# Own order for the opening of a paged-attention, FFN and adapter kernel, with plain fp32 products for tile 0, page numbers first and bulk loads held back

## The reference

```python
# paged attention, 32 query heads on 8 key heads, D = 128, cache of 512 keys + 128 new ones per batch
q, k, v = x @ Wq.T, x @ Wk.T, x @ Wv.T
q, k = rope(rmsnorm(q, q_norm_w), pos), rope(rmsnorm(k, k_norm_w), pos)     # pos = cache_seqlens + 0..127
kc = k_cache[block_table]; vc = v_cache[block_table]                        # 16 pages of 32 keys
scores = where(valid, q @ concat(kc, k).T / sqrt(D), -1e30)
c = softmax(scores) @ concat(vc, v) @ Wo.T
# FFN that zeroes the 688 of 1376 smallest magnitudes per row
s = silu(c @ w_gate.T); s[lower half by |s|] = 0
x = x + (s * (c @ w_up.T)) @ w_down.T
# adapter by batch, then an int4 layer
x = x + (x @ weight[adapter_ids].T) @ unpack_int4(W).T + b
```

## Time and profile before

| | us |
|---|---|
| three runs | 1374.59, 1374.22, 1374.66 |
| median | 1374.59 |
| span of the profiled execution | 1372.6 |
| PE busy | 1356.7 (99%) |
| DVE busy | 1204.1 (88%) |
| ACT busy | 871.6 (64%) |
| POOL busy | 785.0 (57%) |
| granted PE clock | full in all 40 slices |

### The profile page before, as it was taken

How to read it: one execution, slowest core, us unless ns; L and a number is a source line. 1 busy time by engine, 2 the same in 40 slices (tenths; PEclk the granted TensorE clock), 3 DMA queues, 4 the chain that set the end, 5 groups by cost and what they waited for, 6 DMA issues and landing times.

```text
span 1372.6 us, 23448 instructions
## 1 busy us (share of the span) xinstructions
PE 1356.7 (99%) x8015; PEld 1182.3 (86%) x8015; DVE 1204.1 (88%) x2624; ACT 871.6 (64%) x2224; POOL 785.0 (57%) x813
## 2 busy tenths in 40 slices
PE   8899999999999999999999999999999999999998
PEld 6788888888888888888888888888888888888888
DVE  8999898989898989898989898989899987987783
ACT  7777676767676767676767676767777662222221
POOL 7876766676667666766676667666766510111111
PEclk9999999999999999999999999999999999999999
DMA  6111221111112111211111112112121321111212
GB/s 215 48 53 41 59 55 47 43 59 55 47 43 59 54 47 43 58 55 47 43 59 53 49 42 59 55 47 70 49 72 32 110 96 45 47 47 49 76 40 77
DMA packets 34034, 80.46 MB, mean 59 GB/s; under 512 B 10258, under 2 KB 11538, under 8 KB 32498
## 3 DMA queue, kind: packets, MB, share of 16 engines
q1 hardware_dynamic: 17522, 45.29, 10.5%
q0 software_dynamic: 16384, 33.59, 8.4%
HBM read 76.74 MB, written 2.10 MB: 57 GB/s over the span
## 4 chain that ended last, share of the span: by engine, by line
PE 91%; DVE 5%; ACT 2%; issue 1%; POOL 1%; DMA 0%; DVEq 0%; ACTq 0%
PE proj_ps L111 10%; PE proj_ps L113 10%; PE proj_ps L112 10%; PE turn_ps L770 10%; PE score_ps L113 5%; PE score_ps L112 5%; PE score_ps L111 5%; PE value_ps L111 5%; PE value_ps L112 5%; PE value_ps L113 5%; PE gu_ps L111 3%; PE gu_ps L113 3%; PE gu_ps L112 3%; PE out_ps L1035 2%; PE turn_ps L732 2%; PE turn_ps L739 2%
## 5 line engine op out<-in xcount | busy, mean ns | idle before, releaser
L1286 ACT ACTIVATE probs<-probs,shift,rstd 128x640 f32<-128x640 f32 x256 | 234.4, 917 | 123.3 <-DVE shift L1730 122.2
L561 POOL DMA_INDIRECT kg<-kc,idx x256 | 260.1, 1016 | 83.9 <-issue 78.0
L571 POOL DMA_INDIRECT vg<-vc,idx x256 | 260.0, 1016 | 70.7 <-issue 70.7
L1766 DVE TENSOR_TENSOR pt_lo<-turn_ps,pt_hi 128x512 fp32r<-128x512 f32 x320 | 217.4, 685 | 45.2 <-ACT pt_hi L1292 44.8
L1292 ACT ACTIVATE pt_hi<-turn_ps 128x512 fp32r<-128x512 f32 x320 | 187.5, 593 | 90.6 <-PE turn_ps L770 89.3
L1741 DVE CUSTOM_DVE_ANT_0 probs<-score_ps,mask 128x640 f32<-128x640 f32 x256 | 206.8, 822 | 11.9 <-PE score_ps L113 10.1
L579 POOL TENSOR_TENSOR v_lo<-vg,v_hi 128x512 fp32r<-128x512 f32 x64 | 89.1, 1392 | 207.7 <-ACT v_hi L1257 207.7
L770 PE MATMUL turn_ps<-cst,probs 128*128 128x128 f32 x1280 | 191.5, 272 | 0.7 <-DVE qt_lo L1718 0.7
L111 PE MATMUL proj_ps<-w_hi,xt_parts 128*128 128x512 f32 x496 | 188.9, 381 | 0.0
L770 PEld LDWEIGHTS turn_ps<-cst,probs 128*128 128x128 f32 x1280 | 157.2, 141 | 26.9 <-DVE probs L1759 1.0
L113 PE MATMUL proj_ps<-w_hi,xt_parts 128*128 128x512 f32 x496 | 168.1, 339 | 0.0
(11 more groups left out here) (255 smaller groups left out, 3283.4 us busy)
## 6 DMA issues: line engine op xcount, KB each, us to landing
w_raw<-wqkv SPq DMA_DIRECT2D x28, 384.0 KB, 3.2
wo_raw<-wo SPq DMA_DIRECT2D x32, 256.0 KB, 3.0
wa_sb<-wa SPq DMA_DIRECT2D x7, 1024.0 KB, 4.9
kg<-kc,idx POOLq DMA_INDIRECT x256, 2.6
vg<-vc,idx POOLq DMA_INDIRECT x256
wg_raw<-wg SPq DMA_DIRECT2D x2, 1376.0 KB, 6.1
wu_raw<-wu SPq DMA_DIRECT2D x1, 2752.0 KB, 9.6
wd_raw<-wd SPq DMA_DIRECT2D x1, 2560.0 KB, 12.8
```

What stands on the lines that cost most here:

```text
L561: pool.indirect_dma_start(kg[:, b % 2, c, :], None, kc, bass.IndirectOffsetOnAxis(ap=idx[:, s // B % 2, b * NC + c:b * NC + c + 1], axis=0))\
L571: pool.indirect_dma_start(vg[:, b % 2, c, :], None, vc, bass.IndirectOffsetOnAxis(ap=idx[:, s // B % 2, b * NC + c:b * NC + c + 1], axis=0))\
L1286: act.activation(row, row, ACT.Exp, bias=shift[:, h:h + 1], scale=rstd[:, b % 2, h:h + 1], accum_out=sums[:, h:h + 1])\
L1766: dve.tensor_tensor(pt_lo[:, at, :], turn_ps[1 - j % 2][:, :], pt_hi[:, at, :].bitcast(F32), ALU.subtract).then_inc(p_lo_done[j], 1)
```

## The change

The opening (everything before step 1) gets an order of its own on each engine, and other transfers:

- Tile 0's projections of step 0 are made in plain fp32 from x and w as loaded (`first_q`, `first_kv`), four products each, one per 128 rows as each piece of w lands. w of group 0 is loaded and split in five pieces (`W0_PIECES`). x 0 is split only in step 3, as it is next needed in step 8. Three warm-up products on PE instead of six.
- ACT's queue issues page numbers, the small constants, lengths and the identity; SP begins with x 0.
- SP waits for tile 0's cached keys (`k_in[0]`) before it issues x 2 and 3, x 4 to 7 and the output weights.
- ACT normalises one head of four in step 0 and one in step 1 (`BY_ACT`), and the orders of `steps_ahead` and `first_step` differ on all engines. POOL's tables stand elsewhere.
- The angles are reduced with two terms of 2 pi instead of three, and the lengths are read as integers.

Steps 1 to 63 keep their order, but for x 0's split in step 3.

```diff
-TWO_PI = (6.28125, 0.0019350051879882812, 3.0199157663446503e-07)
+TWO_PI = (6.28125, 0.0019353071795864769)
+W0_PIECES = [(slice(k, k + 1), slice(0, GQ)) for k in range(NK)] + [(slice(0, NK), slice(GQ, GW))]
+BY_ACT = (1, 2)
-FILLED = 6
+FILLED = 3
@@ sync
-                    sp.dma_start(cst[:, :], consts[:, 0:C_KEY]).then_inc(const_in, 16)
-                    sp.dma_start(lens_i[:, :], lens).then_inc(const_in, 16)
-                    sp.dma_start(pages_i[:, :], pages).then_inc(pages_in, 16)
                     sp.dma_start(x_raw[:, 0, :, :], xt_b[:, 0, :, :]).then_inc(x_in[0], 16)
-                    for n, (ks, cols) in enumerate(W_PIECES):
-                        if n == LAST_PIECE:
+                    for n, (ks, cols) in enumerate(W0_PIECES):
+                        if n == len(W0_PIECES) - 1:
...
-                    sp.dma_start(key_no, consts[:, C_KEY:C_ALL]).then_inc(key_in, 16)
-                    sp.dma_start(x_raw[:, 2:B, :, :], xt_b[:, 2:B, :, :]).then_inc(x_in[2], 16)
+                    sp.dma_start(key_no, consts[:, C_KEY:C_ALL]).then_inc(table_in, 16)
+                    sp.wait_ge(k_in[0], NC * 16)
+                    sp.dma_start(x_raw[:, 2:4, :, :], xt_b[:, 2:4, :, :]).then_inc(x_in[2], 16)
+                    sp.dma_start(x_raw[:, 4:B, :, :], xt_b[:, 4:B, :, :]).then_inc(x_in[3], 16)
                     for h in range(REP):
                         sp.dma_start(wo_raw[:, h, :], wo[0, :, h, :]).then_inc(wo_in, 16)
@@ tensor
+                    def first_q():
+
+                        pe.wait_ge(x_in[0], 16)
+                        for k in range(NK):
+                            pe.wait_ge(w0_in[k], 16)
+                            last = pe.matmul(proj_ps[:, :], x_raw[:, 0, k, :], w_raw[:, k, 0:GQ], start=k == 0,
+                                             stop=k == NK - 1)
+                        last.then_inc(q_chunks, Q_CALLS)
...
-                        first_projections()
+                        first_q()
+                        first_kv()
+                        pe.wait_ge(ident_in, 16)
+                        turn_cached_k(0, 0)
+                        project_q(1, 1, 0, (0, 1))
                         project_q(1, 1, 0, (2,))
-                        turn_cached_k(0, 0)
                         project_q(1, 1, 0, (3,))
...
@@ scalar
+                    def normalise(s, b, heads):
+
+                        wait(act, recip_done, s + 1)
+                        for h in heads:
+                            row = probs[:, b % 2, h, :]
+                            act.activation(row, row, ACT.Copy, scale=recips[:, h:h + 1]).then_inc(probs_act_done, 1)
...
+                    act.dma_start(pages_i[:, :], pages).then_inc(pages_in, 16)
+                    act.dma_start(cst[:, C_INV:C_KEY], consts[:, C_INV:C_KEY]).then_inc(const_in, 16)
+                    act.dma_start(lens_i[:, :], lens).then_inc(lens_in, 16)
+                    act.dma_start(ident, consts[:, C_ID:C_ID + P]).then_inc(ident_in, 16)
@@ vector
-                        normalise(0, 0, (1, 2, 3))
-                        maxima(1, 1, (0, 1))
+                        normalise(0, 0, (1,))
+                        normalise(0, 0, (2,))
+                        maxima(1, 1, (0,))
+                        maxima(1, 1, (1,))
                         split_probs(0, 0, 0)
...
                         if s < B - 4:
                             split_x(s + 4)
+                        if s == B - 5:
+                            split_x(0)
```

More of the change, by code:

```diff
@@ L656, in table, with steps_ahead @@
                             ALU.mult).then_inc(pool_tables_done[n], 1)
+                    def steps_ahead():
+                        gather_k(0, 0, 0)
+                        gather_k(1, 1, 0)
+                        norms(0, 0)
+                        gather_v(0, 0)
+                        table(0, 1, 0)
+                        norms(1, 1)
+                        gather_v(1, 1, range(0, NC // 2))
+                        gather_k(2, 2, 0)
+                        split_v(0, 0)
+                        table(0, 1, 1)
+                        table(1, 1, 0)
+                        norms(2, 2)
                     def first_step():
+                        gather_v(1, 1, range(NC // 2, NC))
                         gather_v(2, 2)
@@ L697, in project_q @@
                     def project_q(s, b, g, ks):
-                        if b == 0 and ks[0] in (0, 2):
-                            wait(pe, w_lo_done[ks[0] // 2], g + 1)
+                        if b == 0 and g > 0 and ks[0] in (0, 2):
+                            wait(pe, w_lo_done[ks[0] // 2], g)
+                        if s == 1:
+                            wait(pe, w0_lo_done, ks[-1] + 1)
                         if ks[0] == 0:
@@ L1759, in normalise @@
                             last = dve.tensor_scalar(row, row, recips[:, h:h + 1], None, ALU.mult)
-                        if h == REP - 1:
+                        if h == REP - 1 or s < len(BY_ACT) and h == REP - 1 - BY_ACT[s] + (BY_ACT[s - 1] if s else 0):
                             last.then_inc(probs_done, 1)
                     def split_probs(s, b, j):
-                        wait(dve, p_hi_done[j], s + 1)
+                        wait(dve, p_hi_done, NJ * s + j + 1)
                         at = (b + j) % 2
```

246 lines of the change are left out of this document (120 added, 126 removed).

## The result

| | before | after |
|---|---|---|
| median | 1374.33 (5 runs) | 1378.84 (5 runs: 1374.88 to 1379.75) |
| profiled execution, span | 1374.59, 1372.6 | 1374.88, 1373.1 |
| PE, DVE, ACT, POOL busy | 1356.7, 1204.1, 871.6, 785.0 | 1357.3, 1199.9, 873.4, 782.5 |

The ratio is 1.0026, 95% interval 1.0015 to 1.0037; the median is 4.5 us higher. The change is slower where 3.9 us less was forecast. The first profile caught the shortest of the five executions, so that it says little of the other four. I call them the short and the long course; both are read here.

A forecast was written before the change was run, and what follows sets the result against it. PE's waits, mostly for DVE, before step 1's third value product were taken as the bound. Terms 1.0 - 0.8 + 3.9 - 0.2 = 3.9 us cut span 1372.6 to 1368.7; 2.0 around it gave 1370.7 us, range 1368.0 to 1374.4.

The forecast's parts named there:

- Page numbers first: At the start, page numbers issued earlier: index at 3.4 us instead of 4.06, `rstd` 0.9 us sooner.
- Plain fp32: Tile 0's projections on PE as plain products: worth nothing on the path, with about 1.5 us of cover.
- edits at nothing: Angle reduction, w's five pieces, ACT's DMA issues and identity transfer: all done before 18.8 us, so no cost.
- Held bulk: SP's bulk loads wait for tile 0's keys, which land at about 12.2 us instead of 16.7.
- Rival one: Tile 0's keys don't land sooner despite the hold: 1373.3 us, chance 0.12.
- What the hold makes late: Output weights land at 23.1 us, ACT stands about 1 us at `split_wo`; cost 0, with 1.4 us of cover.
- Rival three: Slower: ACT stands at late output weights; 1375.8 us, or 1378 if PE starves too; chance 0.08.
- DVE, first leg: DVE from 18.8 us to the first `pt_lo`, ending at 36.5 against 36.67: 0.2 us gained.
- DVE, second leg: DVE from the first `pt_lo` to the opening's end: 20.05 us instead of 24.0, ending 4.1 us earlier.
- pair waits: DVE instructions with two SBUF operands stalled by POOL arithmetic: 4.2 us in the opening, to go in the second leg.
- rival two: Stalls of DVE beside POOL's arithmetic come back elsewhere: 1372.8 us, or 1375.9 if all of it hits; chance 0.15.
- the join: Third value product of step 1 on PE, forecast at 59.1 us against 62.98; 0.2 us lost there.

The follow-up runs named there:

- wo_first: The changed kernel with the output weights issued ahead of x 4 to 7 after the hold; 1378.25 us.
- again: The changed kernel run again, nothing edited; 1377.74 us, ratio 1.0023 to the kernel before. Its profile caught a longer execution.
- tables_later: The changed kernel with POOL's tables `qb` and `ka` moved from behind `split_v(0, 0)` to behind `gather_v(2, 2)`; 1374.52 us, ratio 1.0005 to the kernel before.
- tables_late: The changed kernel with tables `qb` and `ka` moved behind `gather_v(1, 1)`, ahead of `norms(2, 2)`; 1528.02 us, ratio 1.0012, on a slow chip (before: 1524.57).
- tables_late2: tables_late once more, on another slow chip; 1487.75 us (kernel before: 1486.35).
- spread_later: tables_later with each of the three tables alone between gathers; 1519.37 us, ratio 0.9973, on a slow chip (kernel before: 1524.16).
- again2: The changed kernel unaltered, run again in the last decision group; 1378.39 us, ratio 1.0027 to the kernel before.
- kb_early: The changed kernel with POOL's table `kb` moved from behind `split_v(1, 1)` to ahead of `gather_k(3, 3, 0)`; 1377.47 us, ratio 1.0020 to the kernel before.
- the fourth group: Runs again2, tables_late3 (tables_late repeated), kb_early and tables_later, on one chip beside the kernel before, which took 1374.26 us.
- before_early2: Second run of the kernel before with tables `qa` and `qb` moved directly behind `split_v(0, 0)`; 1490.22 us, ratio 1.0020, on a slow chip.
- small_on_sp: The changed kernel with page numbers, constants and lengths issued by SP ahead of its bulk instead of by ACT; 1374.48 us.

## Why the prediction was wrong

**What bounds the kernel, and how to count: right.** The rest is fixed from the third value product on; the table above bears it out within 0.4 us either way. PE's busy time is as before within 1 us.

**Page numbers first: wrong.** Index forecast at 3.4, measured 5.12. I took the landing time of a transfer issued ahead of all bulk in the trace of before (2.3 us of waiting) for transfers issued beside it, where the constants took 3.8 us. The same three issued on SP ahead of the bulk give 3.58. `rstd`, and with it `rotate_k(0)`, gained 0.2 instead of 0.9 to 1.0.

**Plain fp32, edits at nothing:** worth 0, as said; the keys' products end at 11.9 (forecast 11), ahead of the cached keys.

**Held bulk: mechanism right, size 1.5 us off.** Keys turned at 13.7, not 12.2. Rival one fell: without the hold the last gather, issued at 10.85, is used at 16.82, and with it 10.79 becomes 13.73.
**What the hold makes late: 1.4 to 2 us off, and harmless.** `wo` split at 25.1 and 24.5 in the two courses, not 23.1. It did not set the end, as said (wo_first), though in the short course DVE stood 0.55 us for tile 2's queries behind it. Rival three, my only way to slower, fell.

**DVE, first leg: this step failed.** I had its first `pt_lo` end at 36.5; it ends at 39.95 and 40.1 in the two courses. In again the 3.6 us are three terms:

- 0.8 from the start, `rotate_k(0)` at 19.64, by the late index.
- 0.7 on the way to the reciprocals, forecast for 31.5 (31.2 by my own terms) and measured at 33.02; DVE waits 0.42 and 0.45 us for scores and ahead of `rot_q` where I had 0.35 in all.
- 2.1 at the bias behind the second maximum of tile 1. It reads two SBUF operands. I priced its wait at 1.1 us, by `v_lo(0)` alone, and it stands 3.18, until POOL is through `v_lo` twice, `qb` and `ka`.

The last one is the step that decides. It is in the sentence "tables `qb` and `ka` run at 36.4 to 38.4, beside maxima and `pt_lo`", which puts them at nothing; but between the maxima stand the biases. So the wait that I saw removed at 40.56 was moved to 36.3, and grew. In the short course DVE comes to the bias later, at 38.05 (it was held 0.55 us for queries and 1.2 us for scores, PE's clock being low from 33.7 to 37.1), stands only 1.31, and ends at the same `ka`. Taking the two tables away behind `v_lo(0)` brings the first leg's pair to 38.37 and gives back 3.9 of 4.1 us (tables_later).

That I counted on the end of the first `v_lo` was not without a row. Before:

```profile
35.66 0.33 DVE L1730 SCALAR_TENSOR_TENSOR shift<-row_max,rstd 128x1 f32<-128x1 f32 x1
```

The bias got through at 35.99, where the first `v_lo(0)` ends, though the second follows at once (35.91). So it did in tables_late, tables_late2, tables_later and spread_later (0.35 to 0.37 us), all with a gather or the norm behind the two `v_lo`. With `qb` and `ka` behind them it waited for `ka`'s end each time (again, again2, wo_first and kb_early: 3.18, 2.67, 3.19 and 2.70 us). Why the same boundary lets it through in one order and not in the other, no run shows.

**DVE, second leg: near in the short course** (20.8 against 20.05, most of it the bias at 56.27, which stands 1.51 beside `v_lo(1)` where 0.7 was allowed), **wrong in the usual one.** The pair waits came back, as rival two said with a chance of 0.15: `v_lo(1)` against the rotation products, 2.7 us over their free length. Its upper price, 1375.9, left out what follows such a wait: PE idles 2.5 us, and the clock falls behind it.

**The sum.** 1.0 - 0.8 + 3.9 - 0.2 became 0.2 - 3.5 + 3.2 and nothing at the join in the short course: the first leg's loss eats the second leg's gain. The long one loses another 3.4 us by the join, of which 2.7 are the rotation products' wait; that the rest goes with PE's idling and its low clock is argued, not shown. What sends an execution into one course or the other stays open.

## What to carry to other kernels

When two engines shut each other out, a moved instruction must be priced against everything that the other engine issues in its new place, small instructions above all. Price the wait up to the end of the whole run of such instructions, not of the first alone: four profiles here waited for it in full, though others got through after the first. Read more than one profile of a kernel whose executions scatter more than those of the kernel before (5 us against 1 in the fourth group): the one profile may be the lucky course. And an earlier engine can be the worse one, since it meets others elsewhere.

## What the runs showed that I had not expected

- DVE's normalisation reads one tensor and a column of factors, and is held by POOL's arithmetic all the same: 4.40 us in before_early2 where one alone takes 0.55. The prediction had only instructions with two SBUF operands. The Trainium skill (SBUF — State Buffer, "SBUF: two separate sides") names DVE instructions in a two-port performance mode beside those with two SBUF inputs; the trace agrees with it as far as the 4.40 us go, though no run shows the mode.
- Small transfers land late beside bulk. On ACT's queue, with SP's bulk under way, 4 to 41 KB took 3.4 to 4.1 us from issue to landing and the 64 KB identity 4.5. In small_on_sp the same identity, on the same queue but ahead of the bulk, landed in 2.2 us. So it goes with the bulk, not with the queue.
- PE's granted clock stood at full level all through the opening in the profile of before. In again it fell after 2.51 us of idling, about 1 us after work had come again at 58.41, and stayed at the lower level for 3.4 us.
- One POOL instruction can hold different DVE ones in two profiles of the same kernel: `v_lo(1)`, at 53.85 in again and at 53.63 in again2, held the rotations in the one and the normalisation in the other.
- Chips differ. On one, the granted clock reads 1.00, and PE still gets through fewer products in the same 300 us; on the one where the kernel before takes 1524.57 us it reads 0.97 to 0.99 there (tables_late), which doesn't make up its 11% either. The stretch of tables_late2, then of again:

```profile
300.00:600.00 300.00, 279.21 (x1646) 238.22 (x1646) 241.88 (x563) 194.12 (x518) 182.06 (x192) 1.00 0.16 46
```

```profile
300.00:600.00 300.00, 299.88 (x1815) 264.25 (x1814) 269.83 (x624) 215.03 (x566) 202.71 (x214) 1.00 0.17 50
```

Why is not shown by any run here.
